# Graph layer on one core: TensorE's step with the message sums between the first and the second eight picks

## The reference, cut to what matters

```python
h = jnp.maximum(_layernorm(x, axis=-1), 0.0)
concat = jnp.concatenate([h[src], h[dst], edge_attr], axis=-1)     # 96 + 96 + 64
gates = jax.nn.sigmoid(concat @ W_e + b_e)
messages = jax.nn.softplus(concat @ W_n + b_n)
gated = gates * messages
h_new = jax.ops.segment_sum(gated, dst, num_segments=n)
edge_count = jax.ops.segment_sum(jnp.ones((dst.shape[0],), h.dtype), dst, num_segments=n)
out = x + h + h_new / jnp.clip(edge_count, 1.0, None)[:, None]
```

## Time and profile before

| | |
|---|---|
| median of 3 runs | 749.42 us (746.96 to 753.84) |
| profiled execution | 752.55 us |
| its span on the core | 750.8 us |
| mean granted TensorE clock | 0.86 of full |
| TensorE matmuls busy | 565.8 us (75% of the span) |
| VectorE, ScalarE, GpSimd busy | 552.5, 525.5, 542.9 us |

### The profile page before, as it was taken

One profiled execution on the slowest core, in us unless ns is written; L12 is line 12 of the kernel. 1 busy time (PEld: TensorE's weight loads), 2 busy tenths in 40 slices (PEclk: granted clock), 3 DMA queues, 4 the chain that ended last, 5 costly groups with the idle time before them and its releaser, 6 DMA issues.

```text
span 750.8 us, 14670 instructions
## 1 busy us (share of the span) xinstructions
PE 565.8 (75%) x3832; PEld 537.4 (72%) x3832; DVE 552.5 (74%) x2226; ACT 525.5 (70%) x1330; POOL 542.9 (72%) x404
## 2 busy tenths in 40 slices
PE   1046578888898898888887888889869778788870
PEld 0046577788788788788777887878769778778760
DVE  5766687877877787788787787787787969776550
ACT  0056677778788787786887877878868879688540
POOL 3502238888888888888888888888887878887585
PEclk9999888977987987897898898798897979889885
DMA  7435677978979879888688797897896978867442
GB/s 194 93 80 127 168 166 152 221 153 170 208 140 199 183 156 202 160 182 200 136 201 182 148 209 161 171 210 139 195 188 137 235 143 180 192 95 145 71 49 16
DMA packets 278376, 119.40 MB, mean 159 GB/s; under 512 B 261583, under 2 KB 268824, under 8 KB 278296
## 3 DMA queue, kind: packets, MB, share of 16 engines
q1 hardware_dynamic: 228366, 83.61, 46.4%
q0 software_dynamic: 34576, 18.40, 19.7%
q10 hardware_dynamic: 15354, 16.44, 8.7%
HBM read 71.36 MB, written 48.20 MB: 159 GB/s over the span
## 4 chain that ended last, share of the span: by engine, by line
PE 48%; ACT 20%; issue 14%; DVE 7%; ACTq 4%; POOL 3%; another core or an unknown queue 2%; DMA 1%; POOLq 0%; DVEq 0%
PE pick_ps L976 20%; ACT node_out L478 10%; PE sums_ps L988 6%; PE sums_ps L989 6%; PE z_ps L1041 5%; PE z_ps L1042 4%; PE z_ps L1043 4%; POOL out L411 3%; ACTq L322 3%; PE trans_ps L1021 2%; ACT log1p L550 2%; ACT log1p L545 2%; ACT log1p L540 2%; ACT src_h L508 1%
## 5 line engine op out<-in xcount | busy, mean ns | idle before, releaser
L411 POOL DMA_INDIRECT out<-final,scatter_idx x196 | 314.3, 1604 | 89.0 <-issue 57.3
L397 POOL DMA_INDIRECT edge_x<-in_x,src_idx x196 | 226.3, 1154 | 102.0 <-issue 59.2
L976 PE MATMUL pick_ps<-onehot,node_out 128*96 x1568 | 188.6, 285 | 140.5 <-issue 71.0
L976 PEld LDWEIGHTS pick_ps<-onehot,node_out 128*96 128x96 f32 x1568 | 175.4, 197 | 163.5 <-issue 163.2
L478 ACT ACTIVATE node_out<-node_x,shift,rstd 128x96 f32<-128x96 f32 x637 | 260.8, 457 | 20.6 <-DVE onehot L777 20.6
L821 DVE TENSOR_TENSOR node_out<-node_out,node_x 128x1536 f32<-128x1536 f32 x49 | 86.3, 1760 | 108.3 <-PE pick_ps L976 98.1
L496 ACT ACTIVATE dst_t<-pick_ps 96x336 f32 x98 | 43.8, 447 | 145.8 <-PE pick_ps L976 79.2
L717 DVE BATCH_NORM_STATS2 stats<-node_x 128x6 f32<-128x96 f32 x784 | 143.0, 246 | 1.3 <-issue 1.1
L1041 PE MATMUL z_ps<-w_src,src_t 97*128 97x192 f32 x392 | 106.9, 356 | 0.0
L1042 PE MATMUL z_ps<-w_dst,dst_t 96*128 96x192 f32 x392 | 101.7, 342 | 0.0
L988 PE MATMUL sums_ps<-messages,same 128*128 128x97 f32 x392 | 98.9, 343 | 3.7 <-DVE messages L739 3.7
(11 more groups left out here) (117 smaller groups left out, 589.4 us busy)
## 6 DMA issues: line engine op xcount, KB each, us to landing
node_x<-in_x SPq DMA_DIRECT2D x48, 768.0 KB
out<-node_out SPq DMA_DIRECT2D x48, 768.0 KB
dst_across<-dst_pad ACTq DMA_DIRECT2D x49, 256.0 KB
attr<-in_edge_attr SPq DMA_DIRECT2D x48, 128.0 KB
edge_x<-in_x,src_idx POOLq DMA_INDIRECT x196
out<-final,scatter_idx POOLq DMA_INDIRECT x196
low_across<-low_pad ACTq DMA_DIRECT2D x47, 64.0 KB
node_x<-in_x SPq DMA_DIRECT2D x1, 624.0 KB
```

Source lines behind the costliest of these rows:

```text
L397: nc.gpsimd.indirect_dma_start(out=edge_x[i % NS][:, t, :], out_offset=None, in_=x, in_offset=bass.IndirectOffsetOnAxis(ap=src_idx[:, i * ...
L411: nc.gpsimd.indirect_dma_start(out=out, in_=final[j % FINALS][:, t, :], in_offset=None, out_offset=bass.IndirectOffsetOnAxis(ap=scatter_id ...
L976: last = nc.tensor.matmul(pick_ps[0:D, bass.ds(to[b], WINDOW)], node_out[d % NS][:, h * BLOCKS + b, :], onehot[:, bass.ds(of[b], WINDOW)], ...
```

## The change

Within `step(i)` of TensorE the call `sums(m)` stands ahead of the second half of the picks instead of behind it. Nothing else is changed: the products, their operands and the semaphores are the same, and the other engines' streams stay as they are.

```diff
                     last.then_inc(attr_trans_done, 1)
+                if runs_step(m) and not ends(i, 1):
+                    sums(m)
                 if runs_step(d):
                     picks(d, 1, places_of(2 * d + 1))
-                if runs_step(m) and not ends(i, 1):
-                    sums(m)
                 if runs_step(k):
                     wait(pe, softplus_done, k - 1)
```

## The result

The changed kernel takes 758.14 us (median of 4 runs, 757.73 to 760.18), the kernel before 748.19 beside it (4 runs, 745.71 to 753.84). The ratio is 1.0128, 95% interval 1.0065 to 1.019: slower by some 10 us. The forecast was 771: the side is right, and the forecast difference is twice the measured one.

A forecast was written before the change was run, and what follows sets the result against it. A loop through TensorE's picks and ScalarE's copies, 13.63 us a step, was taken as the bound; 12.9 x 3/7 + 15.0 x 4/7 = 14.1, +0.47 times 45 steps, +21, gives 771 us, range 715 to 805.

The forecast's parts named there:

- The hole moves: TensorE would idle about 2.0 us ahead of the first picks in every step, where it was 0.55, lowering the clock.
- One fall costs 2.1 us: A clock fall from the first picks on makes a step 15.0 us instead of 12.9.
- half clock lasted some 6.7 us: Length of low clock, read from second picks to z's products in the old order, applied from the first picks on.
- four steps in seven: Assumed share of steps with a clock fall, giving 14.1 us a step against 13.63.
- R3: Rival: a clock fall in every step, 15.0 us a step, +62, 811 us; chance 0.12.
- R2: Rival: clock falls late in the first picks, only the sums run slow, about 13.7 a step, 750 us; chance 0.17.
- The Trainium skill's turn that begins cold each time: Loop waiting between two groups of matmuls pays the cold clock every turn; by it every step would take 15.0 us.
- Full clock, 12.9: A step without a clock fall, first picks held to 4.2 us, takes 13.05, shortened to 12.9 us.
- (b): From first picks' start to ScalarE's copy of them, 4.23 us: completion held back until the DMA burst is over.
- R4: Rival: the hold goes with TensorE's order and vanishes, 12.5 to 12.6 us a step, 706 us; with R1 0.20.
- GpSimd would allow it just about: 12.6: GpSimd's scatters, gathers and gaps need 12.6 us a step, just within the 12.9 of full clock.
- R1: Rival: the clock holds, all steps 12.9 us, -33, 717 us; chance 0.20 together with R4.

The follow-up runs named there:

- no_scatter_fill_after: The changed kernel without GpSimd's scatters and with six idle products of 192 columns between second picks and z: 706.48 us (2 runs).
- the two fills: Six idle products a step added to the changed kernel (758.78 us, ratio 1.0176) and to the kernel before (753.41 us, ratio 1.0109).
- small_store: The kernel before, storing only 2 of the 16 node blocks of each chunk: 740.01 us, a single run.
- fill_after: The changed kernel with six idle products of 192 columns between the second picks and z, from step 3 on: 758.78 us, ratio 1.0176.
- the fill: Six idle products of 192 columns a step on TensorE: ratio 1.0176 in the changed kernel, 1.0109 in the kernel before.
- the split: VectorE's node sum as four operations of four blocks: kernel before 733.58 us, ratio 0.982; changed kernel 756.26 us, ratio 1.0123.
- both together: Node sum in four parts plus six idle products: kernel before 719.20 us, ratio 0.9707; changed kernel 723.78 us, ratio 0.9781.
- no_scatter: The kernel before without GpSimd's indirect DMAs that add message sums to the output: 668.06 us, a single run.
- fill_before: The kernel before with six idle products of 192 columns between the transposes and the second picks, from step 3 on: 753.41 us, ratio 1.0109.
- the four kernels of one chip: fill_after 758.78 us, fill_before 753.41, no_scatter 668.06 and small_store 740.01, all run on the same chip.

## Why the prediction was right or wrong

The two orders are bound by different things that happen to cost the same. Before, it is GpSimd with the node sum in its way (13.25 a step with a split node sum, 14.50 with 1.05 us more on it, 12.07 without its scatters; the ratios to the kernel before beside them, 0.982, 1.090 and 0.898, say the same). After, it is TensorE's path from first picks to second picks at a clock that falls in nearly every step (13.66, 13.64, 13.59, whether GpSimd is full, relieved or empty; 12.79 when the clock is kept up). This is shown by the runs. The steady 0.2 us a step between them is the small difference of two limits, and I have no run that splits it further.

- *"The hole moves. This is the term that decides."* Right in kind. The hole of 2.1 to 2.3 us stands ahead of the first picks, z directly behind the second, and the clock is what the order of after costs: 0.80 us a step without scatters, 0.68 with a split node sum (13.64 to 12.96, where GpSimd is next).
- *"One fall costs 2.1 us", "half clock lasted some 6.7 us", "four steps in seven".* This is the step that failed. The falls come in 34 of 42 steps, which is nearly R3, but 26 of them last 3.4 us and not 6.7, have gone before the second picks, and mostly cost 1.0 to 1.2 us against the 12.30 of a step without. Only the 8 that last 10.2 us or more make the slow step of the forecast, 15.67 for my 15.0. The mean of the five steps shown is 13.61 for my 14.1. I had taken the length of half clock from one stretch of the old order and given it to a stretch with other work ahead and behind. In mechanism and number R2 (a fall late in the first picks, 13.7 a step, 750 us) comes nearest, though it kept the change within 1%, and it had 0.17.
- *The Trainium skill's turn that begins cold each time*, "TensorE: Matmul & The Clock Gate", section "HAM oscillation — how this bites in real kernels": the trace agrees on how often, in all but the turns behind a slow one, but the price of most turns is half of what I gave it. The loop that the section describes has waits of 3 to 5 us, longer than the holes here, so it was a weaker support than I took it for.
- *Full clock, 12.9.* 12.30 in the kernel after; 12.79 where every step is held back to the full, in no_scatter_fill_after. The term was right for a held-back step. The full-clock steps in the kernel after aren't held back: their copy comes at about +2.2, and the second picks start at +4.50, straight behind the sums.
- *(b), the burst holds the picks' completion.* Open. The hold is real and stays in the order of after (over 1 us in 28 of 42 steps), so R4 (goes with the order and vanishes) is refuted. (R4's 706 was also counted from the profiled 752.55 and not, like the others, from the median; by that it would be 703.) It needs no scatters. But the same burst stands in the two fills without any hold, so the burst alone doesn't make it, and that it went in small_store proves nothing. I read the 4.23 us as fixed from one step.
- *"GpSimd would allow it just about: 12.6."* Wrong as a bound: 13.6 with the gather's wait for the node sum. I had the gathers at 0.95 each from the earlier trace rows and didn't look at the one in four that takes 1.1 to 2.4. That is why R1's 717 was out of reach: with the clock kept up (fill_after) the kernel stayed at 758.8.
- *"45 steps moved", "the second picks lose 0 to 0.3".* In the first steps, which aren't held back, they lost more, 2 to 4 us in all; I had named such a step and counted "nearly none".
- *The register load, the message wait, VectorE's wait for the sums: nothing.* Nothing speaks against it. They weren't tried alone.

The sum thus came out at +21 for +10: 0.47 a step forecast, 0.2 measured, and 2 to 4 us at the start that weren't in it.

## What to carry to other kernels

When moving work changes nothing in the steady pace, look whether another limit of the same length lies beside the first: here the fill was worth nothing and the split 15 us at best, both together 21, each against the kernel before beside it. Take the duration of an engine's instructions from their spread and not from a typical one: one gather in four was waiting inside its own busy time for VectorE. Price a clock fall by how long it lasts and what stands in it on the path: most lasted 3.4 us and cost about 1.1, those of 10.2 us reached the second picks and cost 3.4. And run the two kernels of a pair on one chip: what no_scatter and small_store seemed to show of the hold was there on their chip without either edit.

## What the runs showed of the hardware

- With six idle products of 192 columns a step the mean granted clock was 0.925 (fill_after, 0.85 in after), 0.934 (fill_before, 0.881 to 0.900 beside it) and 0.973 to 0.979 in the four kernels that also had the split or no scatters.
- In the 42 steady steps of after the clock fell in each of the 34 with 2.1 to 2.3 us of idle TensorE ahead of the first picks and in none of the 8 with 0 to 1.3 us.
- A gather issued by GpSimd during a VectorE addition of two SBUF tensors of 128x1536 doesn't end until 0.9 us behind it (1.85 and 2.35 us for 0.95), though it shows as busy. Scatters that start inside one are late too: in fill_after 27 of 32 took 2.4 to 3.15 us for 1.6. A scatter that was already running didn't delay the addition (1.76 in all 38 such cases of before). Four additions of 128x384 take 1.98 us for 1.76 and let the gather through.
- In before, after and ten other kernels what TensorE reports as finished reaches the others late, in part or nearly all of the steps, in before up to 4.3 us and mostly 2.6, in the stretch in which chunk load and store keep the DMA engines at a share over 1. In the four kernels of one chip it came at once, three of them with the full chunk load and store. The cause is open.
